# Attention scores in a graph kernel: eight multiply-and-sum instructions of 64 columns per step in place of one product over 512 columns and one sum

## The chip, the cores and the metric

The kernel runs on one core of one Trainium2 chip. The metric is the device time of the whole program in microseconds (us). The core has five engines that run side by side and meet only through semaphores: TensorE (PE in the profile), VectorE (DVE), ScalarE (ACT), GpSimd (POOL) and SyncE (SP). Each takes its instructions in the order in which they are written. In front of each engine stands a sequencer that reads the instructions, does register work and semaphore waits, and hands the rest on.

## The reference

The program is one graph-attention layer (with its own feed-forward part) and, behind it, a mixture of eight experts over the same 3,125 nodes of 256 features. The change touches the scores of the attention alone: for each of 53,125 edges and each of 4 heads, the product of a query row and a key row of 64 numbers each is summed.

```python
qi = q[dst]                                   # [53125, 4, 64]
kj = k[src]
vj = v[src]
alpha = jnp.sum(qi * kj, axis=-1) / jnp.sqrt(jnp.float32(D))      # D = 64
m = jax.ops.segment_max(alpha, dst, num_segments=n)
ex = jnp.exp(alpha - m[dst])
denom = jax.ops.segment_sum(ex, dst, num_segments=n)
a = ex / (denom[dst] + 1e-16)
out = jax.ops.segment_sum(a[..., None] * vj, dst, num_segments=n)
```

## The kernel before

There are four stages, one behind the other: `project` makes the rows of keys and values and sorts out which edges belong to which block of 128 nodes; `attend` runs over the edges; `mlp` and `experts` are dense layers, mostly products on TensorE. The change is in `attend`.

`attend` walks over 232 steps of 256 edges (`LT` = 2 tiles of 128 edges, one edge per partition). Eight steps (`CP`) make a chunk, four chunks (32 steps, `RING`) a round. The first round is written out, six rounds are a loop on each engine (`Fori(1, ROUNDS)`), and the last 8 steps and the tail of the pipeline are written out again. The work of one step, by engine:

- POOL fetches two tiles of key-and-value rows from HBM by index (`indirect_dma_start`, L665) into `ring`. It may run 8 steps ahead: it waits on `s_prod` for the step whose slot it refills. Once a chunk it also copies the indices (`idx`, L649) and the run starts (`stc`), after waits on `s_alpha` and `s_mp`.
- PE expands the queries of the block to one row per edge (six products into `psQ`, L735; four buffers, `NQ`, freed by `s_prod`), and 16 steps later sums the weighted values per node (`psA`, L758).
- DVE does the scores. L940 multiplies `psQ` (in PSUM) by the keys in `ring`, 128 partitions by 512 columns, into `prod`. L980 sums `prod` over runs of 64 columns into 8 numbers per partition: 2 tiles by 4 heads. Between the two stand other pieces of the step: parts of the running maximum over the previous chunk (`maximum`, parts 0, 1 and 2), the one-hot rows `oh` (L958), and the addition of `psA` to the result `acc` (L974, named `k_acc` in the trace). Once a chunk come the mask `ohT` (L827) and the rescaling of `acc` (L998).
- ACT takes the exponents and scales the values (eight instructions, L715).

At the start of every step DVE's sequencer loads the number of the block from memory into a register (`value_load`), which L974 of that step uses; the instructions behind it are handed on only after that. The order on each engine is written out by hand; nothing is scheduled by a planner. DVE writes a step in this order (parts left out):

```python
blk = nc.vector.value_load(brow[0:1, bass.ds(b, 1)], min_val=0, max_val=NB - 1)
...
dve.wait_ge(s_kv[jj], 16 * LT * (cc + 1))
dve.wait_ge(s_qe, step + 1)
...                          # product, L940
maximum(i, j, 0)
...                          # one-hot rows, L958
maximum(i, j, 1)
...                          # addition to acc, L974
maximum(i, j, 2)
...                          # sum, L980
```

In the first round DVE and ACT also split the projected queries into three parts (`remainder`, `lowest`, L833 and L837), one block per step.

Of the kernel before, what the change touches and what calls it, by code (L numbers as in the profile page):

```python
# [37 lines left out]
LT = 2  # L38
# [465 lines left out]
def attend(nc, ctx, io, keep):  # L504

    c = ExitStack()
    with c:
# [6 lines left out]
        def sem(name):  # L514
            return ctx.enter_context(nc.semaphore(name))
# [48 lines left out]
        s_oht, s_noh = sem("s_oht"), sem("s_noh")  # L564
        s_qe, s_prod, s_alpha = sem("s_qe"), sem("s_prod"), sem("s_alpha")
        s_mv, s_mp = sem("s_maxv"), sem("s_maxp")
# [70 lines left out]
        def _(pool):  # L637
            def at(i, j, fresh):
# [4 lines left out]
                if j % CP == 0:  # L643
                    if not (fresh and j < 2 * CP):
                        pool.wait_ge(s_alpha, CP * (cc - 1))
                        held(pool, s_turn[1])
                        pool.wait_ge(s_mp, NT * (cc - 2) + T_IN)
                        held(pool, s_turn[1])
# [169 lines left out]
        def _(dve):  # L818
# [28 lines left out]
            def maximum(i, j, part):  # L847
# [11 lines left out]
                if at == (0, 0):  # L859
                    dve.wait_ge(s_alpha, CP * m + CP)  # L860
                    nc.vector.tensor_tensor(alm[:, :, :], alpha[:, mpar, :, :],
                                            valN[:, bass.ds(W * m, W)].unsqueeze(1).broadcast_to([P, H, W]), ALU.add).then_inc(s_mv, 1)
# [64 lines left out]
            def at(i, j, fresh):  # L927
# [6 lines left out]
                if live(i, j, fresh):  # L934

                    dve.wait_ge(s_kv[jj], 16 * LT * (cc + 1))
                    dve.wait_ge(s_qe, step + 1)
                    if not (fresh and j < 2):
                        dve.wait_ge(s_alpha, step - 1)
                    nc.vector.tensor_tensor(prod[:, j % 2, :].rearrange("p (k d) -> p k d", k=LT),  # L940
                                            psQ[j % NQ][:, :].rearrange("p (k d) -> p k d", k=LT),
                                            ring[:, LT * jj:LT * jj + LT, q + 1, 0:HID], ALU.mult).then_inc(s_prod, 1)
                if now:
# [31 lines left out]
                if now:  # L975
                    maximum(i, j, 2)
                if live(i, j, fresh):

                    dve.wait_ge(s_prod, step + 1)
                    nc.vector.tensor_reduce(alpha[:, q % 2, :, LT * jj:LT * jj + LT].rearrange("p h w -> p w h"),  # L980
                                            prod[:, j % 2, :].rearrange("p (k h d) -> p k h d", k=LT, h=H), AX.X, ALU.add
                                            ).then_inc(s_alpha, 1)
                if fresh and QEARLY + j < NB:
# [831 lines left out]
```

## Time and profile before

| what | value |
|---|---|
| time, median of 3 runs | 1516.69 us (1516.41 to 1521.55) |
| profiled execution, its own time | 1517.29 us |
| its span, first to last instruction | 1515.5 us |
| DVE busy over the span | 1104.2 us (73%), 2825 instructions |
| PE busy | 1272.6 us (84%) |
| POOL busy | 848.6 us (56%) |
| ACT busy | 773.8 us (51%) |
| first L940 and last L980 | 110.9 us and 755.3 us |
| mean granted TensorE clock | 0.950 |

The shares are means over stages with different limits, so they say little about `attend`, which lies between some 110 and 780 us. What bounds it is read from the views of that stretch alone. A row of the timeline gives the start, the time from the start of the operation to its acknowledged end, and the instruction. On DVE one instruction often starts before the recorded end of the one before it, so the time that an instruction takes from the engine is the distance between two starts, and not its recorded length.

### The profile page before, as it was taken

The numbers are of one execution on the slowest core, as the hardware profiler recorded it, in microseconds if no ns is written. First come the engines' busy times: TensorE is split into PE (matmuls) and PEld (weight loads), VectorE is DVE, ScalarE is ACT, GpSimd is POOL, SyncE is SP. The second block draws the span as 40 slices with busy tenths as digits, with TensorE's granted clock in tenths as the row PEclk, the third lists the DMA queues.
The fourth block names the chain that finished last, engine by engine and source line by source line (L and its number), as shares of the span: only waits on it lengthen the run. The fifth ranks groups of instructions, "written<-read, shape, count | busy, mean of one in ns | idle before, by whom it ended". The sixth has DMA issues, their size and how long they took to land. (4 is left out here: it accounts for less than half of the span.)

```text
span 1515.5 us, 29900 instructions
## 1 busy us (share of the span) xinstructions
PE 1272.6 (84%) x7188; PEld 992.9 (66%) x7189; DVE 1104.2 (73%) x2825; ACT 773.8 (51%) x2480; POOL 848.6 (56%) x932
## 2 busy tenths in 40 slices
PE   5899777776767767777749999968899999999998
PEld 2434455454544545545537777757799999999998
DVE  4647999898988989988973555457956656566665
ACT  1155877786776767776732222213334435344443
POOL 2146777777777777777610111025656657566665
PEclk8999999899999999999988999968999999999999
DMA  5377777777777777777630111141110010100000
GB/s 182 117 220 221 223 215 204 214 221 217 205 216 206 209 217 216 212 210 214 172 108 22 53 52 52 33 136 42 60 36 19 1 52 0 35 17 0 18 2 16
DMA packets 83555, 184.24 MB, mean 122 GB/s; under 512 B 11611, under 2 KB 46262, under 8 KB 83454
## 3 DMA queue, kind: packets, MB, share of 16 engines
q0 software_dynamic: 37632, 124.28, 28.9%
q1 hardware_dynamic: 44438, 57.57, 11.5%
q10 hardware_dynamic: 1384, 1.32, 0.3%
q8 instruction: 31, 0.51, 0.1%
q14 instruction: 70, 0.57, 0.1%
HBM read 165.93 MB, written 17.18 MB: 121 GB/s over the span
## 5 line engine op out<-in xcount | busy, mean ns | idle before, releaser
L665 POOL DMA_INDIRECT ring<-kv_rows,idx x464 | 477.7, 1029 | 167.7 <-issue 127.7
L715 ACT ACTIVATE ring<-ring 128x64 f32<-128x64 f32 x1800 | 435.7, 335 | 0.9
L1533 ACT ACTIVATE hf<-psF,k_scT 128x320 f32<-128x320 f32 x320 | 197.8, 618 | 223.6 <-PE psF L1566 215.2
L735 PE MATMUL psQ<-k_q,ohT 128*128 x1392 | 210.3, 286 | 90.1 <-issue 89.9
L758 PE MATMUL psA<-ring,oh 128*128 128x260 f32 x928 | 255.3, 400 | 3.8 <-DVE k_acc L974 3.7
L735 PEld LDWEIGHTS psQ<-k_q,ohT 128*128 128x128 bf16 x1392 | 122.3, 99 | 148.5 <-issue 122.8
L1500 POOL TENSOR_TENSOR h2l<-hf,h2h 128x320 fp32r<-128x320 f32 x160 | 148.7, 944 | 115.2 <-DVE h2h L1709 115.2
L940 DVE TENSOR_TENSOR prod<-psQ,ring 128x512 f32<-128x512 f32 x232 | 158.6, 684 | 60.0 <-DMA ring<-kv_rows,idx 34.0
L758 PEld LDWEIGHTS psA<-ring,oh 128*128 128x128 f32 x928 | 166.5, 200 | 26.2 <-issue 4.2
L1500 POOL TENSOR_TENSOR h1l<-hf,h1h 128x320 fp32r<-128x320 f32 x160 | 148.3, 950 | 59.9 <-DVE h1h L1709 59.9
L980 DVE TENSOR_REDUCE alpha<-prod 128x8 f32<-128x512 f32 x232 | 155.8, 671 | 0.2
L1709 DVE CAST h2h<-hf 128x320 fp32r<-128x320 f32 x160 | 90.7, 583 | 62.7 <-ACT hf L1533 62.6
L1709 DVE CAST h1h<-hf 128x320 fp32r<-128x320 f32 x160 | 83.7, 529 | 56.3 <-ACT hf L1533 56.1
L1566 PE MATMUL psO<-wh,h2l 128*128 128x256 f32 x400 | 110.7, 297 | 9.2 <-DVE o L1698 8.4
L1698 DVE SCALAR_TENSOR_TENSOR o<-psO,wt,o 128x256 f32<-128x256 f32 x200 | 92.6, 479 | 33.4 <-PE psO L1566 32.1
L1566 PE MATMUL psO<-wl,h2h 128*128 128x256 f32 x400 | 107.3, 289 | 0.0
L1566 PE MATMUL psF<-xh,wl 128*128 128x320 f32 x320 | 100.9, 322 | 0.0
L1566 PE MATMUL psF<-xl,wh 128*128 128x320 f32 x320 | 99.7, 318 | 0.0
L1566 PE MATMUL psF<-h1h,wl 128*128 128x320 f32 x320 | 97.6, 313 | 0.0
L1566 PE MATMUL psF<-h1l,wh 128*128 128x320 f32 x320 | 96.3, 309 | 0.0
L974 DVE TENSOR_TENSOR k_acc<-k_acc,psA 128x260 f32 x232 | 93.7, 404 | 2.8 <-PE psA L758 1.0
L1130 POOL TENSOR_SCALAR ve<-mv 128x5 f32<-128x5 f32 x10 | 3.3, 329 | 164.7 <-DVE mv L1254 100.1
(234 smaller groups left out, 2332.4 us busy)
## 6 DMA issues: line engine op xcount, KB each, us to landing
ohT<-step_destinations SPq DMA_DIRECT2D x29, 512.0 KB, 4.3
ring<-kv_rows,idx POOLq DMA_INDIRECT x464, 3.8
kv_rows<-kvst SPq DMA_DIRECT2D x25, 260.0 KB, 2.1
we<-in_L_ffn_W SPq DMA_DIRECT2D x16, 256.0 KB, 3.0
residual<-qst SPq DMA_DIRECT2D x25, 128.0 KB, 3.6
resin<-residual SPq DMA_DIRECT2D x5, 640.0 KB, 6.6
after_graph_layer<-x SPq DMA_DIRECT2D x5, 640.0 KB, 5.7
xres<-after_graph_layer SPq DMA_DIRECT2D x5, 640.0 KB, 4.4
```

The costliest lines, as they stand in the source:

```text
L665: nc.gpsimd.indirect_dma_start(out=ring[:, LT * (j % CP) + k, j // CP:j // CP + 2, :].rearrange("p t e -> p (t e)"), out_offset=None, in_= ...
L715: last = nc.scalar.activation(row[:, 0:D], row[:, 0:D], ACT.Copy, scale=row[:, D:HW_])
L735: last = nc.tensor.matmul(psQ[j % NQ][:, k * HID:(k + 1) * HID], ohT[par][:, w * P:(w + 1) * P], q3[:, part, bass.ds(blk, 1), :].rearrange ...
L758: last = nc.tensor.matmul(psA[sj % NA][0:BP, 0:HALFW], oh[:, sj % NO, k, :], ring[:, LT * (sj % CP) + k, sj // CP, :], start=(k == 0), sto ...
L940: nc.vector.tensor_tensor(prod[:, j % 2, :].rearrange("p (k d) -> p k d", k=LT), psQ[j % NQ][:, :].rearrange("p (k d) -> p k d", k=LT), ri ...
L974: nc.vector.tensor_tensor(row, row, psA[sj % NA][0:BP, 0:HALFW], ALU.add).then_inc(s_acc, 1)
L980: nc.vector.tensor_reduce(alpha[:, q % 2, :, LT * jj:LT * jj + LT].rearrange("p h w -> p w h"), prod[:, j % 2, :].rearrange("p (k h d) -> ...
L1500: nc.gpsimd.tensor_tensor(low, hf[:, n, 0:b - a], high, ALU.subtract).then_inc(s_rl, 1)
L1533: nc.scalar.activation(hf[:, n, 0:b - a], psF[n][:, 0:b - a], ACT.Relu, bias=scT[:, 2 * layer - 1, col + m:col + m + 1], scale=scT[:, 2 * ...
L1566: mm = nc.tensor.matmul(out, ws(k)[iw], xs(k)[ix], start=(at == 0), stop=(at == len(n) - 1))
L1698: nc.vector.scalar_tensor_tensor(out=o[:, u, :], in0=ps, scalar=wt[:, u, e:e + 1], in1=o[:, u, :], op0=ALU.mult, op1=ALU.add).then_inc(s_c ...
L1709: nc.vector.tensor_copy(high, hf[:, n, 0:b - a]).then_inc(s_rh, 1)
```

## The change

The product and the sum become eight instructions, each of which multiplies 64 columns of `psQ` by 64 columns of `ring`, writes the products to `prod`, and writes their sum to one column of `alpha`. They stand together where the product stood. The semaphore `s_prod` is now signalled once, behind the last of the eight, and takes the place of `s_alpha` for those that waited for the sums.

```diff
@@ gpsimd @@
-                        pool.wait_ge(s_alpha, CP * (cc - 1))
+                        pool.wait_ge(s_prod, CP * (cc - 1))
@@ maximum, part 0 of a chunk's first step @@
-                    dve.wait_ge(s_alpha, CP * m + CP)
+                    dve.wait_ge(s_prod, CP * m + CP)
@@ vector, at(i, j, fresh) @@
                     dve.wait_ge(s_kv[jj], 16 * LT * (cc + 1))
                     dve.wait_ge(s_qe, step + 1)
-                    if not (fresh and j < 2):
-                        dve.wait_ge(s_alpha, step - 1)
-                    nc.vector.tensor_tensor(prod[:, j % 2, :].rearrange("p (k d) -> p k d", k=LT),
-                                            psQ[j % NQ][:, :].rearrange("p (k d) -> p k d", k=LT),
-                                            ring[:, LT * jj:LT * jj + LT, q + 1, 0:HID], ALU.mult).then_inc(s_prod, 1)
+                    for k in range(LT):
+                        for h in range(H):
+                            a = h * D
+                            last = nc.vector.tensor_tensor_reduce(
+                                out=prod[:, j % 2, k * HID + a:k * HID + a + D], in0=psQ[j % NQ][:, k * HID + a:k * HID + a + D],
+                                in1=ring[:, LT * jj + k, q + 1, a:a + D], scale=1.0, scalar=0.0, op0=ALU.mult, op1=ALU.add,
+                                accum_out=alpha[:, q % 2, h, LT * jj + k:LT * jj + k + 1])
+                    last.then_inc(s_prod, 1)
...
-                if live(i, j, fresh):
-
-                    dve.wait_ge(s_prod, step + 1)
-                    nc.vector.tensor_reduce(alpha[:, q % 2, :, LT * jj:LT * jj + LT].rearrange("p h w -> p w h"),
-                                            prod[:, j % 2, :].rearrange("p (k h d) -> p k h d", k=LT, h=H), AX.X, ALU.add
-                                            ).then_inc(s_alpha, 1)
```

In the built program each `tensor_tensor_reduce` is two DVE instructions: the one that multiplies and sums, and one that reads the sum out into a single column of `alpha`. The rows below are DVE's, from the second step of a chunk (j % 8 = 1) to the start of the third, in the kernel before. `ISA x2`, `REGISTER_ALU` and rows with a wait alone are the sequencer's; `TENSOR_LOAD k_brow` is the load of the block number.

```order
L958 ISA [waits s_agg]
L958 TENSOR_TENSOR oh<-k_iotaF,k_dstR 128x256
L974 ISA [waits s_rescaled,s_acc,s_agg]
L974 TENSOR_TENSOR k_acc<-k_acc,psA 128x260
L980 TENSOR_REDUCE alpha<-prod 128x2x4 [waits s_prod]
L933 ISA
L933 TENSOR_LOAD k_brow
L933 ISA x2
L937 REGISTER_ALU [waits s_kv2]
L940 TENSOR_TENSOR prod<-psQ,ring 128x512 [waits s_alpha,s_qe]
```

The same place in the changed kernel, where L961 and L977 are the former L958 and L974; the pair of rows of L941 stands eight times in a row.

```order
L961 ISA [waits s_agg]
L961 TENSOR_TENSOR oh<-k_iotaF,k_dstR 128x256
L977 ISA [waits s_rescaled,s_acc,s_agg]
L977 TENSOR_TENSOR k_acc<-k_acc,psA 128x260
L933 ISA
L933 TENSOR_LOAD k_brow
L933 ISA x2
L937 REGISTER_ALU [waits s_kv2]
L941 ISA prod,alpha<-psQ,ring 128x64 [waits s_qe]
L941 ISA alpha 128x1
```

The sum of 512 columns no longer stands between the addition to `acc` and the load of the block number; 16 instructions stand behind the load where one stood. On POOL nothing moves, and only the semaphore's name changes, as in this piece of the difference at the start of a chunk in the loop (the copy of the indices and the wait ahead of it):

```order
 L665 DMA ring<-kv_rows,idx 128x520
 L645 REGISTER_ALU
-L647 ISA [waits s_alpha]
+L647 ISA [waits s_prod]
 L649 ISA [waits s_maxp]
 L649 COPY idx<-k_srcI 128x16
```

The waits of PE and POOL on `s_prod` for a free buffer stay where they were; the signal itself now comes behind the last sum.

## Rows read from the trace of the kernel before

**Rows 1.** The page, costliest groups: the product and the sum.

```profile
L940 DVE TENSOR_TENSOR prod<-psQ,ring 128x512 f32<-128x512 f32 x232 | 158.6, 684 | 60.0 <-DMA ring<-kv_rows,idx 34.0 <-issue 20.7 <-DVE alpha L980 2.2
L980 DVE TENSOR_REDUCE alpha<-prod 128x8 f32<-128x512 f32 x232 | 155.8, 671 | 0.2
```

**Rows 2.** Busy time by window: four rounds of the loop, second and sum.

```profile
core 0: us, PE busy (x) PEld busy (x) DVE busy (x) ACT busy (x) POOL busy (x), PEclk, DMA share, GB/s
375.75:466.26 90.51, 65.28 (x372) 44.26 (x372) 79.02 (x217) 64.67 (x268) 67.94 (x72) 0.96 0.74 212
sum 360.14, PE 267.06 PEld 180.27 DVE 316.49 ACT 258.70 POOL 269.69; mean PE 66.77 PEld 45.07 DVE 79.12 ACT 64.68 POOL 67.42
```

**Rows 3.** DVE's waits, 120 to 780 us: total, times, longest.

```profile
DVE prod L940 <- DMA ring<-kv_rows,idx: 34.0, 36, 2.8
DVE prod L940 <- issue: 20.7, 10, 4.1
DVE qst L833 <- ACT k_q L683: 5.5, 6, 1.4
DVE prod L940 <- DVE alpha L980: 2.2, 6, 0.5
```

**Rows 4.** DVE's timeline around 412 us: start, length, line, instruction.

```profile
411.56 0.67 DVE L980 TENSOR_REDUCE alpha<-prod 128x8 f32<-128x512 f32 x1
412.16 0.67 DVE L940 TENSOR_TENSOR prod<-psQ,ring 128x512 f32<-128x512 f32 x1
412.75 0.20 DVE L919 TENSOR_TENSOR dif<-alm,psM 128x64 f32<-128x64 f32 x1
412.88 0.41 DVE L958 TENSOR_TENSOR oh<-k_iotaF,k_dstR 128x256 f32<-128x256 f32 x1
...
419.23 0.69 DVE L940 TENSOR_TENSOR prod<-psQ,ring 128x512 f32<-128x512 f32 x1 [2.05 <-DMA ring<-kv_rows,idx]
```

**Rows 5.** POOL's timeline: first gathers of two chunks in a row.

```profile
413.50 1.30 POOL L665 DMA_INDIRECT ring<-kv_rows,idx  x1 [1.04 <-DVE prod L940]
415.10 0.95 POOL L665 DMA_INDIRECT ring<-kv_rows,idx  x1 [0.30 <-issue]
416.36 0.94 POOL L665 DMA_INDIRECT ring<-kv_rows,idx  x1 [0.30 <-issue]
...
436.22 1.30 POOL L665 DMA_INDIRECT ring<-kv_rows,idx  x1 [1.04 <-DVE prod L940]
```

**Rows 6.** DVE's timeline, short instructions in a row.

```profile
410.25 0.27 DVE L909 TENSOR_SCALAR oh<-k_iotaF,k_dstR 1x128 f32<-1x128 f32 x1
410.45 0.14 DVE L912 COPY bin_<-psR 64x1 f32<-64x1 f32 x1
410.52 0.40 DVE L958 TENSOR_TENSOR oh<-k_iotaF,k_dstR 128x256 f32<-128x256 f32 x1
```

**Rows 7.** DVE's timeline, four and five short instructions merged.

```profile
22.84 0.36 DVE L354 BATCH_NORM_AGGREGATE mv<-st 128x2 f32<-128x6 f32 x4
...
788.29 0.66 DVE L1254 BATCH_NORM_AGGREGATE mv<-st 128x2 f32<-128x6 f32 x5 [0.15 <-DVE st L1249]
```

**Rows 8.** DVE's timeline, a sum directly behind its product.

```profile
119.54 0.68 DVE L940 TENSOR_TENSOR prod<-psQ,ring 128x512 f32<-128x512 f32 x1
120.25 0.69 DVE L980 TENSOR_REDUCE alpha<-prod 128x8 f32<-128x512 f32 x1
```

**Rows 9.** DVE's timeline, instructions around loads of the block number.

```profile
408.84 0.67 DVE L980 TENSOR_REDUCE alpha<-prod 128x8 f32<-128x512 f32 x1
409.50 0.69 DVE L940 TENSOR_TENSOR prod<-psQ,ring 128x512 f32<-128x512 f32 x1
...
421.24 0.42 DVE L998 TENSOR_TENSOR k_acc<-k_acc,fac 128x260 f32 x1
421.78 0.69 DVE L940 TENSOR_TENSOR prod<-psQ,ring 128x512 f32<-128x512 f32 x1
```

**Rows 10.** DVE's timeline, the first product of a round.

```profile
466.26 0.69 DVE L940 TENSOR_TENSOR prod<-psQ,ring 128x512 f32<-128x512 f32 x1 [3.67 <-issue]
```

More of the change, by code:

```diff
@@ L564, in attend @@
         s_oht, s_noh = sem("s_oht"), sem("s_noh")
-        s_qe, s_prod, s_alpha = sem("s_qe"), sem("s_prod"), sem("s_alpha")
+        s_qe, s_prod = sem("s_qe"), sem("s_prod")
         s_mv, s_mp = sem("s_maxv"), sem("s_maxp")
```

## The prediction

> **What bounds the kernel now.** The change lives in `attend`, so I read the group table first, to see how often its two instructions run: 232 products of 684 ns and 232 sums of 671 ns [rows 1]. Next I took the busy time of four rounds of the loop, to see which engine is fullest there. A round lasts 360.14 / 4 = 90.0 us. DVE is busy for 79.1 us of it, POOL for 67.4, PE for 66.8 and ACT for 64.7 [rows 2]. DVE is therefore the fullest by busy time, with 10.9 us of idle time a round. DVE's waits say what that idle time is: in `attend` 34.0 us for the gathered rows to arrive and 20.7 us of "issue", in which nothing in the profile is waited for [rows 3]. The issue time sits mostly at the loop's back edge, with 3.67 us ahead of a round's first product [rows 10]; there are five such places, of 3.6 to 4.1 us.
>
> The wait for rows has a second engine behind it. POOL starts a gather every 1.26 us, since 0.30 us of issue lies ahead of each, and 22.72 us lie between the first gathers of two chunks [rows 5]. Sixteen gathers at 1.26 are 20.2 us, and the copies and the wait at the head of a chunk are the rest. DVE needs 79.1 / 4 = 19.8 us for a chunk, and it catches up with POOL about once a chunk, as in the 2.05 us ahead of the product at 419.23 [rows 4]. So two engines set the pace nearly together: DVE with its instructions and its back edge, 79.1 + 4 = 83 us a round, and the gathers with some 88 us. Whatever DVE gains is lost to the gathers, and what it loses is free only for the first 5 us a round or so. That matters more here than the shares of the whole span.
>
> **What is removed.** The price of an instruction in a full queue is the distance between starts. The sum at 411.56 is followed by the product at 412.16, and that by the next instruction at 412.75 [rows 4]. That is 0.60 and 0.59 us, so a step gives back 1.20 us. The wait for `s_alpha` ahead of the product and that for `s_prod` ahead of the sum go too. In a steady step both had long been met, so I cost them at nothing.
>
> **What is added.** Sixteen instructions a step: eight of 64 columns that read PSUM and SBUF, and eight that write one column. The trace has neither kind under its own name. For the first the nearest row is `dif`, 64 columns from PSUM and SBUF, with 412.88 - 412.75 = 0.13 us between starts [rows 4]. A 128-column instruction takes 0.20 and a one-column copy from PSUM takes 0.07 [rows 6], whose middle is 0.135. For the second the nearest row is that one-column copy, at 0.07. A pair then costs 0.205 us and eight pairs 1.64 us. This is the lower bound: it supposes that the readout starts without waiting for the end of the sum, and that the sequencer keeps up.
>
> Whether it keeps up is the first open cost. Four tiny instructions behind long ones took 0.36 us together, so (0.36 - 0.15) / 3 = 0.07 each, but five that came behind an idle moment took 0.66, so (0.66 - 0.15) / 4 = 0.127 each [rows 7]. I read the first as instructions that stood ready and the second as the pace at which they can be handed on. Sixteen in a row are more than were ever seen to stand ready, and at 0.127 they take 2.03 us. A block thus costs 1.64 to 2.03 us. I take the middle, 1.82, since the long instructions ahead of the block let the sequencer run ahead for its first part only. Against the 1.20 removed that is +0.62 us a step.
>
> **The Trainium skill on the same price.** The row says 0.13 us for 64 columns out of PSUM [rows 4]. The Trainium skill, page "VectorE: DVE Perf Modes", section on the TRN2 errata, charges 120 cycles plus one per column for a PSUM source and 58 plus one for an SBUF source, at 0.96 GHz. By an estimate from that page a pair is 0.192 + 0.061 = 0.253 us, eight are 2.03 us, and with the rest of my sum unchanged the program would take 1686 us. The row disagrees with the PSUM figure (0.13 against 0.19), and I go by the row.
>
> **What is moved.** The sum of `prod` stood between the addition to `acc` and the load of the block number, and its 0.60 us hid that load. Even that was barely enough: at 408.84, behind very short instructions, the next product came 0.66 us later and not 0.60. Behind the rescaling at 421.24, with a load of its own just before it, it came 0.54 us later [rows 9], where instructions of that width otherwise follow each other at 0.34. So a load that has only an addition of 260 columns over it can show through by up to 0.20 us. In the new order that addition always stands there, but no load directly ahead of it; so 0 to 0.20, and I take 0.08 us a step. Together the step grows by 0.62 + 0.08 = 0.70 us on DVE, which is 232 x 0.70 = 162 us.
>
> The signal `s_prod` comes 1.2 us later within the step. PE has four `psQ` buffers and POOL eight steps of `ring`, so both keep at least three steps of cover, some 8 us. I cost it at nothing; without that cover it would be up to 1.2 us a step. ACT's and PE's 65 to 67 us a round leave them far from binding.
>
> **What is absorbed.** With DVE slower than the gathers, its waits for them vanish: 34.0 us, with 2.2 that are put down to the sum of the step before. In the first round DVE also waits 5.5 us behind ACT's splitting of the queries, and that covers the longer block there [rows 3]. That makes 41.7 us. The 20.7 us of issue stay. The code of a round grows by 14 instructions a step, and if fetching at the five back edges doubled with it, that would be 18 us more [rows 10]. I leave this out of the sum and in the range.
>
> **Sum.** On the profiled execution's own time: 1517.3 + 162 - 41.7 = 1638 us. The runs' median lies 0.6 below that execution, so I say 1637. By rounds: 79.1 + 32 x 0.70 + 4.1 = 105.6 us against 90.0, over 7.25 rounds 113 us, which agrees.
>
> **The rivals.**
>
> *The readout waits for the end of its sum.* A sum waited for by semaphore started 0.71 us behind the start of a product that lasted 0.68, that is 0.03 behind its end [rows 8]. If the engine holds the readout back in the same way, a pair is 0.20 (the recorded length of 64 columns) + 0.03 + 0.07 = 0.30 us, and eight are 2.40. The step grows by 1.28 us, so 297 - 42 = +255, about 1772 us. For it speaks that the readout needs the last column's sum. Against it speaks that the overlap of 0.07 to 0.08 us between neighbours looks like the acknowledgement of the write, which the readout does not need. The Trainium skill, page "VectorE: DVE Perf Modes", section on two Vector instructions with no wait between them, counts an instruction that writes out its accumulator as two and holds one back only when start quadrants differ. All operands here start at partition 0, so by that rule nothing is held; no run so far shows it.
>
> *Everything one after the other.* If the next sum also waits for the readout's recorded end, the pair is 0.23 + 0.14 + 0.03 = 0.40 us, eight are 3.2, the step grows by 2.08 us, and the time is 1517 + 483 - 42 = 1958 us.
>
> *Not slower: the gathers hide it.* The block may grow by 41.7 / 232 = 0.18 us a step before the time moves, since DVE then only fills its waits for POOL. That needs a pair of no more than (1.20 + 0.18) / 8 = 0.17 us with the load hidden. A 64-column instruction of 0.135 leaves 0.04 for the readout, below the 0.07 of the shortest instruction in the trace. If the readout cost nothing at all, DVE would gain 0.12 us a step and the gathers would keep it: the time would stay within a few us of 1517.
>
> **How the numbers follow.** Pairs of 0.205 to about 0.26 us with my other terms: 0.58. The readout waits: 0.24. Everything in turn: 0.12. Hidden by the gathers: 0.05, of which 0.01 falls to a gain. The last 0.01 is for costs outside these. The likeliest case spans 1517 + 232 x 0.44 - 42 = 1577 (lower bound, load hidden) to 1517 + 232 x (0.83 + 0.20) - 42 = 1714, and with the back edges 1732. The range runs from 1565 to 1785 so as to take in the waiting readout; outside lie the fully serial case and the hidden one. Faster, the same and slower, at a bound of 0.5%, are 0.01, 0.04 and 0.95; 0.5% is about what a measurement of this kernel can tell.
>
> **What would show it.** In the new profile the 232 rows each of L940 and L980 are replaced by 1856 pairs. I expect starts of pairs 0.20 to 0.25 us apart, blocks of about 1.8 us, a round of about 106 us, DVE busy for nearly all of it, no waits for gathered rows, and POOL waiting on `s_prod` in every step. Ahead of each block I expect a short issue gap of about 0.1 us. The prediction is wrong if pairs lie 0.3 us apart or more, if the gap ahead of each block is several tenths, or if the back edges have grown.

## The result and the profile after

The changed kernel takes 1565.03 us (median of 4 runs, 1564.44 to 1571.32) against 1516.55 us (1516.06 to 1521.55) of the kernel before: a ratio of 1.0332, 95% interval 1.0305 to 1.036. It is slower by 48 us, where 120 were forecast. The profiled span is 1563.8 us. The granted clock is 0.963 and was 0.950, so the clock is no cause. A ratio is always against the kernel before of the same series of measurements, since that kernel took 1513 to 1519 us in some series, called quiet below, and 1621 to 1636 us in others, called busy, for a reason that isn't known and that is not the chip, as some expectations guess (chips 8 and 11 each gave both).

The page of the changed kernel, costliest groups (columns as in [rows 1]), has the 1856 pairs in place of the product and the sum:

```profile
L941 DVE CUSTOM_DVE_ANT_0 prod<-psQ,ring 128x64 f32<-128x64 f32 x1856 | 289.2, 220 | 91.3 <-issue 82.3
L941 DVE DVE_READ_ACCUMULATOR2_ANT alpha<- 128x1 f32 x1856 | 153.2, 83 | 1.0 <-issue 0.2
```

By these sums the pairs cost 442 us where product and sum cost 314. That reading is wrong, since the recorded ends overlap. The timeline of the changed kernel around 430 us gives the distances between starts:

```profile
428.71 0.39 DVE L977 TENSOR_TENSOR k_acc<-k_acc,psA 128x260 f32 x1
429.03 0.20 DVE L879 COPY inh<-carry 1x64 f32<-1x64 f32 x1
429.69 0.22 DVE L941 CUSTOM_DVE_ANT_0 prod<-psQ,ring 128x64 f32<-128x64 f32 x1 [0.47 <-issue]
429.84 0.08 DVE L941 DVE_READ_ACCUMULATOR2_ANT alpha<- 128x1 f32 x1
429.84 0.22 DVE L941 CUSTOM_DVE_ANT_0 prod<-psQ,ring 128x64 f32<-128x64 f32 x1
429.98 0.08 DVE L941 DVE_READ_ACCUMULATOR2_ANT alpha<- 128x1 f32 x1
...
430.85 0.08 DVE L941 DVE_READ_ACCUMULATOR2_ANT alpha<- 128x1 f32 x1
430.85 0.14 DVE L882 COPY cin<-psR 64x1 f32<-64x1 f32 x1
430.92 0.41 DVE L961 TENSOR_TENSOR oh<-k_iotaF,k_dstR 128x256 f32<-128x256 f32 x1
...
431.64 0.39 DVE L977 TENSOR_TENSOR k_acc<-k_acc,psA 128x260 f32 x1
431.96 0.41 DVE L889 TENSOR_TENSOR_SCAN B<-nrow,F 64x128 f32<-64x128 f32 x1
432.62 0.23 DVE L941 CUSTOM_DVE_ANT_0 prod<-psQ,ring 128x64 f32<-128x64 f32 x1 [0.25 <-issue]
...
434.90 0.14 DVE L904 TENSOR_TENSOR fd<-tails,back 1x4 f32<-1x4 f32 x1
435.57 0.22 DVE L941 CUSTOM_DVE_ANT_0 prod<-psQ,ring 128x64 f32<-128x64 f32 x1 [0.53 <-issue]
```

Two things are to be seen. First, a readout starts at the very moment at which the next sum starts (429.84 twice), and takes nothing from it. A pair is 0.145 us and the block of eight goes from 429.69 to 430.85, 1.16 us, which is also the median of all blocks. The 1.20 us that were removed paid for it. Second, ahead of each block there is a stop with nothing waited for. From the small copy `inh` to the block it is 0.66 us, where such a copy is followed at 0.10 in places without a load. It is 0.66 behind `B` (0.33 without a load) and 0.67 behind `fd` (0.08). Between these instructions and the block stand the load of the block number with its range check, and semaphore waits, to none of which the view puts these stops down.

The trace also has the sequencer's own rows (DVEq), with the shortest, the median and the longest in ns. These are the ones of the load in the changed kernel, 120 to 830 us:

```profile
L933 DVEq FUSED_REGOPS  x394: 53/190/190, 159.9 to 829.9; - x197
L933 DVEq TENSOR_LOAD <-k_brow x232: 297/307/329, 159.6 to 829.5; - x116
L933 DVEq SEQ_ASSERT  x231: 23/23/23, 160.2 to 829.1; - x116
```

The load itself is 0.31 us, and behind it stand 0.19 and 0.02 us of range check (the rows of 53 ns stand ahead of it). By the starts of these rows, the block starts 0.76 to 0.84 us behind the start of the load at each of the eight steps of a chunk (medians by step), whatever instruction stands last. The load itself starts between 0.32 us before and 0.11 us after that last instruction. In the kernel before it starts 0.14 to 0.76 us before the sum at the seven steps where the sum stands last, and the sum's 0.60 us then run over the rest of it.

The waits of DVE in the changed kernel, 120 to 830 us, have it in one line, against 10 times and 20.7 us in [rows 3]:

```profile
DVE prod L941 <- issue: 82.3, 169, 5.0
DVE k_acc L995 <- DVE k_acc L977: 11.5, 28, 0.6
```

The second line is the rescaling: it has a load of its own, which the sum covered before and which now stands directly behind the addition. No line for gathered rows is left; 34.0 us stood there before. The busy time by window, four rounds of the loop in the changed kernel, second and sum as in [rows 2]:

```profile
397.53:496.13 98.60, 64.79 (x372) 43.55 (x372) 80.58 (x665) 64.78 (x268) 66.31 (x72) 0.98 0.68 195
sum 392.59, PE 260.79 PEld 174.72 DVE 323.18 ACT 259.15 POOL 264.22; mean PE 65.20 PEld 43.68 DVE 80.79 ACT 64.79 POOL 66.06
```

A round takes 392.59 / 4 = 98.15 us and took 90.04: 8.1 us more. I split both rounds by distances between starts on DVE. The instructions themselves come to some 77.3 us and were 78.4. Stops for the load, with those inside the blocks, are some 16.5 us and were 1.4. Waits for gathered rows are 0 and were 6.1. The back edge is 4.5 and was 3.9 (4.57, 4.48, 4.96, 4.63 and 3.70 us at the five places). That gives -1.1 + 15.1 - 6.1 + 0.6 = 8.5, near the 8.1 measured. The loss is one item, and part of it was absorbed.

### The profile page after: what moved, and what is told of

The parts are those of the page before. It is cut to its first block and busy times, and to the rows that moved or that the text cites. A ratio compares the mean times of both kernels' runs of the same rounds, so it can differ in the third digit from the quotient of the medians.

```text
span 1563.8 us, 32956 instructions
## 1 busy us (share of the span) xinstructions
PE 1261.1 (81%) x7188; PEld 982.9 (63%) x7189; DVE 1110.3 (71%) x6073; ACT 775.1 (50%) x2480; POOL 835.9 (53%) x932
## 5 line engine op out<-in xcount | busy, mean ns | idle before, releaser
L665 POOL DMA_INDIRECT ring<-kv_rows,idx x464 | 464.9, 1002 | 198.1 <-issue 127.1
L941 DVE CUSTOM_DVE_ANT_0 prod<-psQ,ring 128x64 f32<-128x64 f32 x1856 | 289.2, 220 | 91.3 <-issue 82.3
L735 PE MATMUL psQ<-k_q,ohT 128*128 x1392 | 205.1, 281 | 113.7 <-issue 96.3
L758 PE MATMUL psA<-ring,oh 128*128 128x260 f32 x928 | 249.3, 393 | 3.3 <-DVE k_acc L977 3.0
L758 PEld LDWEIGHTS psA<-ring,oh 128*128 128x128 f32 x928 | 161.8, 195 | 28.4 <-issue 6.5
L941 DVE DVE_READ_ACCUMULATOR2_ANT alpha<- 128x1 f32 x1856 | 153.2, 83 | 1.0 <-issue 0.2
L961 DVE TENSOR_TENSOR oh<-k_iotaF,k_dstR 128x256 f32<-128x256 f32 x232 | 95.4, 411 | 0.0
L977 DVE TENSOR_TENSOR k_acc<-k_acc,psA 128x260 f32 x232 | 93.4, 403 | 2.0 <-PE psA L758 1.0
```

Of the source, the lines that this page charges most:

```text
L665: nc.gpsimd.indirect_dma_start(out=ring[:, LT * (j % CP) + k, j // CP:j // CP + 2, :].rearrange("p t e -> p (t e)"), out_offset=None, in_= ...
L735: last = nc.tensor.matmul(psQ[j % NQ][:, k * HID:(k + 1) * HID], ohT[par][:, w * P:(w + 1) * P], q3[:, part, bass.ds(blk, 1), :].rearrange ...
L758: last = nc.tensor.matmul(psA[sj % NA][0:BP, 0:HALFW], oh[:, sj % NO, k, :], ring[:, LT * (sj % CP) + k, sj // CP, :], start=(k == 0), sto ...
L941: last = nc.vector.tensor_tensor_reduce(out=prod[:, j % 2, k * HID + a:k * HID + a + D], in0=psQ[j % NQ][:, k * HID + a:k * HID + a + D], ...
L961: nc.vector.tensor_tensor(oh[:, sj % NO, :, :], iotaF[:, 0:BP].unsqueeze(1).broadcast_to([P, LT, BP]), dstR[:, bass.ds(LT * bo, LT)].unsqu ...
L977: nc.vector.tensor_tensor(row, row, psA[sj % NA][0:BP, 0:HALFW], ALU.add).then_inc(s_acc, 1)
```

## The experiments

The theory to test (cover theory): DVE's sequencer starts the load only when it has handed on the instruction ahead. It comes there hardly ahead of the engine, so nothing long is queued by then. The 0.60 us of the removed sum used to hide the load. The rival: 14 more instructions a step cost time in themselves, in issue or in fetching.

### The order alone

The kernel before, with the sum of step j-1 directly behind the product of step j. No instruction is added, but the load now stands behind the same small instructions as in the changed kernel.

```diff
@@ vector, behind the product @@
+                if not (fresh and j == 0) and (live(i, j, fresh) or (isinstance(i, int) and RING * i + j == STEPS)):
+                    jb = (j - 1) % RING
+                    qb, jjb = jb // CP, jb % CP
+                    dve.wait_ge(s_prod, step)
+                    nc.vector.tensor_reduce(alpha[:, qb % 2, :, LT * jjb:LT * jjb + LT].rearrange("p h w -> p w h"),
+                                            prod[:, jb % 2, :].rearrange("p (k h d) -> p k h d", k=LT, h=H), AX.X, ALU.add
+                                            ).then_inc(s_alpha, 1)
@@ vector, end of the step @@
-                if live(i, j, fresh):
-
-                    dve.wait_ge(s_prod, step + 1)
-                    nc.vector.tensor_reduce(alpha[:, q % 2, :, LT * jj:LT * jj + LT].rearrange("p h w -> p w h"),
-                                            prod[:, j % 2, :].rearrange("p (k h d) -> p k h d", k=LT, h=H), AX.X, ALU.add
-                                            ).then_inc(s_alpha, 1)
```

> The kernel before, with the sum over the product of step j-1 placed directly behind the product of step j; nothing is left out, and the same instructions run. The addition to acc now stands directly ahead of the load of the block number, as in the changed kernel. Cover theory: the changed kernel is slow because the 0.60 us sum no longer hides the load, so this one should show the same gap of some 0.3 us ahead of each product (0.67 us from the start of the addition to the start of the product) and take 1550 to 1565 us. Sequencer theory: the changed kernel is slow because DVE's sequencer has 14 more instructions to hand on in each step and never gets ahead; here it has no more than before, runs ahead during product and sum, and the time stays at 1517 to 1525 us.

> The kernel before with the sum of step j-1 directly behind the product of step j, again, since its first run met the slower chip; nothing is left out. There its trace already had 0.69 us from the start of the last short instruction to the product, where 0.08 to 0.33 would be the distance without a load. Summed over a round that is some 11 us of idle time, of which the gathers' slack takes 6. Cover theory: on a chip that runs the kernel before in 1517 us this takes 1545 to 1560 us, a ratio of 1.02 to 1.03, with no change in any instruction. If the number of instructions is what counts, the ratio is below 1.005.

> The kernel before with the sum of step j-1 moved directly behind the product of step j, so that what stands ahead of the load of the block number in the next step is the same short instruction as in the changed kernel, while the scores are still one product and one sum: no instruction is added. Alone in its call. If the loss of the changed kernel is the uncovered load of the block number (cover theory), this kernel loses most of it too: distances of 0.65 to 0.7 us from the last short instruction to the product, 9 to 13 us more a round less what the gathered rows gave (6 a round), 1545 to 1565 us, ratio 1.02 to 1.03. If the loss comes from the number of instructions (14 more a step), it stays within 0.5% of the kernel before: 1512 to 1525 us.

The first two were in busy series: 1627.66 against 1623.08 us, ratio 1.0019 (0.9993 to 1.0045), and 1624.37 against 1621.24, ratio 1.001 (0.9983 to 1.0037). The stops were there (0.69 to 0.70 us behind `inh` and `fd`), the total didn't show them. The third was in a quiet one: **1560.22 against 1518.33 us, ratio 1.0269 (1.0213 to 1.0324)**. The timeline of that run, around 409 us:

```profile
409.68 0.21 DVE L902 TENSOR_TENSOR iv<-back,k_nxt 1x64 f32<-1x64 f32 x1
409.82 0.14 DVE L904 TENSOR_TENSOR fd<-tails,back 1x4 f32<-1x4 f32 x1
410.52 0.69 DVE L940 TENSOR_TENSOR prod<-psQ,ring 128x512 f32<-128x512 f32 x1 [0.56 <-issue]
411.12 0.68 DVE L947 TENSOR_REDUCE alpha<-prod 128x8 f32<-128x512 f32 x1
```

It stops 0.70 us behind `fd` like the changed kernel, with the old instructions. So the order alone costs 42 us, where the change costs 48. The two are not made of quite the same pieces. Here the load is still covered at two of eight steps: it starts 1.04 and 1.12 us ahead of the addition that stands last, against 0.17 and 0.24 in the changed kernel, which loses some 0.5 us a chunk more by it. In return this order has a wait that the changed kernel has not: once a chunk `alm` waits for the sum directly ahead of it and starts 0.82 us behind it, where other instructions start 0.59 behind, which is some 7 us of the 42. The waits of that run, 120 to 830 us:

```profile
DVE prod L940 <- issue: 76.4, 143, 3.8
```

### Fewer loads

The changed kernel and the kernel before, each with the block number loaded once a chunk. Seven of eight steps then add to a block that isn't chosen by their own number: that choice is left out.

```diff
+            kept = []
...
-                    blk = nc.vector.value_load(brow[0:1, bass.ds(b, 1)], min_val=0, max_val=NB - 1)
+                    if jj == 0 or (fresh and j == ADD_LAG) or not kept:
+                        kept[:] = [nc.vector.value_load(brow[0:1, bass.ds(b, 1)], min_val=0, max_val=NB - 1)]
+                    blk = kept[0]
```

> The changed kernel with the block number for the addition loaded once in eight steps instead of in each; the seven steps behind it add to the block of the first, so the choice of the block is left out for them. Both theories: with seven of eight loads gone the gap ahead of the block goes, the issue idle falls from 82 to some 30 us, and the gathers set the pace: 1505 to 1520 us. If the load is not the cost and the sixteen instructions are slow to fetch or to hand on by themselves, the time stays above 1545 us.

> The changed kernel with one load of the block number a chunk, again on what I hope is the chip of the first measurement; the choice of the block is left out for seven steps of eight. Cover theory: all but one in eight of the stops go, some 14 of 15 us a round, the gathers set the pace, and the time is 1500 to 1520 us (ratio 0.99 to 1.00). If the instructions themselves are supplied too slowly, gaps appear inside the blocks and the ratio stays at 1.02 or more.

> The changed kernel with one load of the block number a chunk instead of one a step, again; the choice of the block is left out for seven steps of eight. Where instructions are supplied fast enough: no gap ahead of the blocks, ratio to the kernel before 0.99 to 1.005. Where they are not: the gaps move into the blocks and the ratio stays near that of the changed kernel. If the load is not the cost, the ratio equals that of the changed kernel on either chip.

> The kernel before with one load of the block number a chunk for its addition, instead of one a step; the choice of the block is left out for seven steps of eight. In the kernel before the load is hidden behind the sum of 0.60 us, so the time stays within 1% of the kernel before, whose pace the gathers set. If loads cost there too, it gains more than 1%.

> The changed kernel with one load of the block number a chunk, run alone this time, since the kernel before took 1517 us where one kernel was sent alone and 1620 to 1636 us in all runs of several together. The choice of the block is left out for seven steps of eight. If the stops for the load are the whole loss: 1500 to 1520 us, a ratio of 0.99 to 1.00. If the loss is in the supply of the instructions: gaps inside the blocks, a ratio of 1.02 or more.

The quiet series decides for the result: **1506.11 against 1517.54 us, ratio 0.9933 (0.9907 to 0.9958)**. With seven of eight of these loads gone the changed kernel takes 0.7% less than the kernel before, a small difference but clear of its interval. The distances to the block fall to 0.10 behind `inh`, 0.08 behind `fd` and 0.33 behind `B`, and the gathered rows are waited for again. DVE's waits, 120 to 830 us:

```profile
DVE prod L945 <- issue: 28.4, 6, 6.0
DVE prod L945 <- DMA ring<-kv_rows,idx: 15.5, 12, 3.1
```

In busy series it is otherwise. There this kernel took 1689.06 against 1623.08 us (1.039), 1687.22 against 1621.24 (1.0412) and 1706.92 against 1636.07 (1.0432, 1.0399 to 1.0464), though its stops ahead of the blocks are gone. The kernel before with one load a chunk took 1639.67 against 1636.07 (1.0005, 0.9977 to 1.0032). So in busy series taking the loads away gives nothing that can be seen, and the kernel with the pairs stays 4% behind.

> The changed kernel itself, beside the next two on the same chip, since the first four experiments met a chip on which the kernel before took 1623 us instead of 1517. If the loss is a fixed amount of work on DVE, the ratio to the kernel before is 1.03 on any chip. If it is a matter of how fast instructions are supplied, the ratio on the slower chip is larger, 1.04 to 1.08, with issue idle inside the blocks.

The changed kernel, run unchanged in that same series, took 1702.18 against 1636.07 us, 1.0393 (1.0357 to 1.0429). DVE's waits of that run, 120 to 830 us, name a place that the quiet run hardly has, a stop between sum and readout (alpha, 0.2 us in all in the page above):

```profile
DVE prod L941 <- issue: 99.2, 181, 4.4
DVE alpha L941 <- issue: 30.9, 47, 1.2
```

This looks like the rival theory, that the instructions come too slowly, but the runs don't show it. The same pairs at the end of the step cost only 1.4 to 1.7% in busy series, and with twice the pairs the stops between sum and readout were fewer (25.4 us in 52 places against 37.4 in 56, over the whole of `attend`; both edits follow). What costs the 4% in busy series is open.

### The block at the end of the step

The eight pairs stand where the sum stood, so that they should cover the load of the next step.

> The changed kernel, with the block of eight pairs moved from the head of the step to its end, where the sum stood; nothing is left out. Cover theory: the block of 1.16 us now stands between the addition and the load of the block number and hides the load, so the issue idle falls to some 25 us and the time to 1510 to 1525 us. Sequencer theory: the order does not matter, since the sequencer works through the 16 short instructions about as slowly as the engine does and arrives at the load with nothing queued; the time stays at 1555 to 1575 us and the gap only moves to the instruction behind the load.

> The changed kernel with the block at the end of the step, again. With the range check kept, the sequencer stops behind the block, whose last instructions take 0.07 us each, so only what stands ready covers the stop. From the trace of the version without the check (96.0 us a round against 98.2 of the changed kernel) I expect 1550 to 1565 us, a ratio of 1.02 to 1.03. If a block of 1.16 us covered the stop as the sum of 0.60 did, it would be 1510 to 1520 us.

> The changed kernel with both remedies: the block of pairs at the end of the step, where the sum stood, and the block number of the addition loaded without its range check, so that nothing stops for it before the addition; nothing is left out. If stopping for the load is what the change costs, this one loses it all: on the chip of the first measurement 1500 to 1520 us, where the gathers set the pace, and on the slower chip a ratio of 1.00 to 1.01 against 1.039 of the changed kernel. If the number of instructions is the cost, the ratio stays at 1.03 or above.

Both runs with the range check were in busy series: 1647.91 against 1623.08 us, 1.014 (1.0095 to 1.0185), and 1648.91 against 1621.24, 1.0168 (1.0132 to 1.0203). That is some 2.4% less than the changed kernel of such a series. The third also leaves the range check away (the load without `min_val` and `max_val`) and was in a quiet series: 1549.97 against 1517.52 us, 1.0209 (1.0182 to 1.0237). I had expected more of it. Its timeline around 433 us shows where the stops went:

```profile
433.36 0.15 DVE L829 TENSOR_SCALAR noh<-ohT 128x1 f32<-128x1 bf16 x1
433.88 0.42 DVE L965 TENSOR_TENSOR k_acc<-k_acc,psA 128x260 f32 x1 [0.37 <-issue]
```

Without bounds at the load, the check is made where the number is used: the sequencer's rows of up to 0.19 and of 0.02 us now belong to the line of the addition, which followed `noh` at 0.19 us and now follows at 0.52. The experiment had moved a stop, not removed it.

> The changed kernel with the block number of the addition loaded in every step but without its range check, so that the first instruction that needs the loaded number is the addition itself and not the check directly behind the load; nothing of the computation is left out. If the load only costs because the sequencer stops for its answer, the gap ahead of the block shrinks from 0.3 us to 0.1 or less and the time falls to 1505 to 1530 us. If the load itself holds the sequencer, or if the number of instructions is what counts, the time falls by less than 20 us, to 1545 or more. A stop that moves to the addresses of the addition would show as idle time ahead of the addition.

> The changed kernel with the load of the block number in its own place, only without the two range checks on the number. Alone in its call, for the share of the checks in the 48 us. Earlier it ran among others, where its distances from the last short instruction to the pairs were 0.36 us against 0.66 us with checks. By that, 0.3 us a step or up to 9 us a round comes back at the steps where nothing else waits: 1525 to 1550 us, ratio 1.005 to 1.02. If the place alone makes the cost, it stays at 1555 to 1570 us.

The same edit in the changed order was measured twice, both times in busy series: 1684.16 against 1623.08 us, 1.0339 (1.0287 to 1.0391), and 1693.27 against 1634.12, 1.0366 (1.0316 to 1.0416). Its distances from `inh`, `B` and `fd` to the block are 0.36 to 0.37 us where they were 0.66, and from the start of the load to the block it is 0.48 where it was 0.77. So some 0.3 us of the stop is the check. What is left of it is 0.26 behind `inh` (0.36 less the 0.10 without a load), 0.30 behind `fd` and 0.04 behind `B`. Here too the check came back ahead of the addition, which follows `noh` at 0.52 us. The total of this version in a quiet series wasn't measured.

### Twice the pairs

Every pair is issued twice; the first eight write to buffers that nobody reads (`pr` and `al` take the places of `prod` and `alpha`).

```diff
-                    for k in range(LT):
+                    for pr, al, k in [(prod2, alpha2, k) for k in range(LT)] + [(prod, alpha, k) for k in range(LT)]:
...
```

> The changed kernel with every pair issued twice, the first eight into buffers that nobody reads; nothing is left out. It prices eight pairs in a queue that is already running. At 0.145 us a pair, as in the trace of the changed kernel, a step grows by 1.16 us and the program by 232 x 1.16 = 269 us, a ratio near 1.21. If the sequencer falls behind in a long run of short instructions, as the prediction had it, a pair costs 0.20 to 0.25 and the ratio is 1.28 to 1.34.

It took 1870.99 us against 1636.07 in a busy series, 1.1428 (1.1375 to 1.1481). I had expected a ratio near 1.21. The block of sixteen takes 2.37 us in the median, 0.148 a pair. The sequencer therefore keeps up with at least 32 instructions in a row at 0.074 us each. That settles the price of the pair. The total is 169 us above the changed kernel of the same series and not 232 x 1.2 = 278; some of the block presumably lay beside other stops of that series, which no run separates.

### How a load is hidden

Three more versions are complete and without the range check at load or use. First, seven loads in a row behind the first block of a chunk, kept in registers (`number`, a load without its check, is shown with the next version).

```diff
...
+                if jj == 0 and not fresh:
+                    for t in range(1, CP):
+                        if live(i, j + t, fresh, ADD_LAG):
+                            kept[j + t] = number(step + t - ADD_LAG)
```

> The changed kernel, complete, but the block numbers of a chunk's next seven steps are loaded one behind the other right behind the chunk's first block of pairs and kept in seven registers, without range checks; the rescale takes its number from there too where it lies in them. The question is whether seven loads in a row cost seven stops or one. If each waits for the one before (0.35 us or more each), a chunk loses 2.5 us in one place, 10 us a round, and the kernel stays near 1545 to 1560 us, ratio 1.02 or more. If they overlap, a chunk loses some 0.5 to 0.8 us in one place, and the kernel comes to what the version with one load a chunk took plus a few us: 1503 to 1518 us, ratio 0.992 to 1.0.

It took 1552.53 against 1515.26 us, 1.0255 (1.0238 to 1.0273). The timeline at such a place:

```profile
340.98 0.09 DVE L947 DVE_READ_ACCUMULATOR2_ANT alpha<- 128x1 f32 x1
344.13 0.23 DVE L861 TENSOR_TENSOR alm<-alpha,k_valN 128x64 f32<-128x64 f32 x1 [3.06 <-issue]
```

Seven loads stop DVE for 3.06 us, or 0.44 each. They don't overlap: the sequencer's rows show each at 0.30 to 0.34 us, and none starts before the one ahead has ended.

Then one load a step, for the next step, directly behind this step's block. The rescaling takes the number that is already there.

```diff
+            def number(b):
+                return nc.s_assert_within(nc.vector.value_load(brow[0:1, bass.ds(b, 1)]), 0, NB - 1,
+                                          skip_runtime_bounds_check_because="the plan holds block numbers below NB")
...
-                    blk = nc.vector.value_load(brow[0:1, bass.ds(b, 1)], min_val=0, max_val=NB - 1)
+                    blk = kept.pop(j) if j in kept else number(b)
...
                     last.then_inc(s_prod, 1)
+                    if j + 1 < RING and live(i, j + 1, fresh, ADD_LAG):
+                        kept[j + 1] = number(step + 1 - ADD_LAG)
...
-                    blk = nc.vector.value_load(brow[0:1, bass.ds(br, 1)], min_val=0, max_val=NB - 1)
+                    blk = kept[j + 1] if j + 1 in kept else number(br)
```

> The changed kernel, complete, but the block number of the next step is loaded right behind this step's block of pairs and kept in a register, without range checks, and the rescale uses the number that is already there. One load a step as before the edit, only in another place. If a load stops VectorE wherever the work queued ahead of it is short (cover theory: the block of pairs is issued at nearly the engine's pace, so little is queued), the stop moves behind the block at 0.3 to 0.4 us: 1530 to 1550 us, ratio 1.01 to 1.02. If only the short instruction ahead and the check made it dear, it is hidden: below 1517 us.

It took **1497.18 against 1513.09 us, 0.9896 (0.9842 to 0.995)**, less than I had expected and less than both kernels, 1% below the kernel before. Its timeline, around 405 us:

```profile
405.05 0.07 DVE L947 DVE_READ_ACCUMULATOR2_ANT alpha<- 128x1 f32 x1
405.29 0.21 DVE L893 COPY heads<-psR 1x64 f32<-1x64 f32 x1 [0.17 <-issue]
405.45 0.43 DVE L969 TENSOR_TENSOR oh<-k_iotaF,k_dstR 128x256 f32<-128x256 f32 x1
...
406.46 0.14 DVE L904 TENSOR_TENSOR fd<-tails,back 1x4 f32<-1x4 f32 x1
406.53 0.20 DVE L947 CUSTOM_DVE_ANT_0 prod<-psQ,ring 128x64 f32<-128x64 f32 x1
```

The block follows `fd` at 0.07 us. Behind the block the load shows as 0.17 us here. In the median over the loop it shows as nothing at two of the eight steps and as 0.08 to 0.30 us at the other six, 4.4 us a round in all, where the uncovered loads cost some 16.5. The sequencer is ahead of the engine by part of the block when it comes to the load, which is enough for most of the cover and not for all. The waits and the windows of four rounds (sum) of this kernel:

```profile
DVE prod L947 <- issue: 18.8, 5, 4.1
...
sum 350.73, PE 259.23 PEld 175.52 DVE 318.41 ACT 259.13 POOL 260.91; mean PE 64.81 PEld 43.88 DVE 79.60 ACT 64.78 POOL 65.23
```

Ahead of the blocks only the five back edges are left of the issue time, and a round is 350.73 / 4 = 87.7 us. DVE waits for gathered rows only 2.6 us in all, so DVE sets this pace and not the gathers.

Last, the same load in the kernel before, behind its product.

> The kernel before, complete, with the same load of the block number one step ahead, without range checks, here right behind the product (0.60 us on VectorE). It says whose gain the version with the pairs and the load ahead has. Before has its load behind the sum, where it costs 0.60 us from the sum to the next product in 0.60 us of sum, nothing; behind the product of 0.60 us it should be covered as well (0.35 to 0.4 us without a check). So the cover theory expects no more than 0.5% from the kernel before, 1510 to 1520 us. If range checks or the placing help any kernel by themselves, this one gains the same 1% as the pairs with the load ahead did: 1495 to 1503 us.

It took 1515.97 against 1517.11 us, 0.9992 (0.9969 to 1.0016): no change. Its waits for gathered rows are 49.8 us, against 34.0:

```profile
DVE prod L946 <- DMA ring<-kv_rows,idx: 49.8, 35, 3.2
DVE prod L946 <- issue: 6.9, 2, 3.5
```

Most of that growth is a matter of names: three back edges of 2.9 to 3.2 us are put down to the rows here and stood under "issue" before. Without them the waits for rows are 40.5 us, 6.5 more. DVE gained about as much: the product follows the rescaling at 0.34 us in place of 0.54, once a chunk, some 6 us in all. So what DVE gained there, it waited for POOL. The 1% of the version above comes with the pairs, given that their load is hidden. Why that version isn't held back by the gathers in the same way is open in part. Its chunks of gathers start 22.1 us apart in the median, against 22.7 in the kernel before, and the difference lies at the head of a chunk: the last gather ahead of it takes 0.95 us in the median and took 1.52, and the first behind it 0.97 and 1.30. No run says why.

## Why the prediction was right and wrong

**The direction, and what bounds.** DVE and the gathers set the pace nearly together, and the change put DVE behind: right. The waits for rows vanished as forecast, 34.0 and 2.2 us [rows 3].

**What is removed.** 1.20 us a step: right, by the same way of reading starts.

**Sixteen instructions a step: this step failed.** I took 1.82 us for the block, 1.64 to 2.03. It measured 1.16, so the term is -0.04 us a step in place of +0.62. Even my lower bound charged each readout 0.07 us of its own, as if it were a one-column copy [rows 6]. The readout starts with the next sum and costs nothing. The upper bound came from the pace of five instructions behind an idle moment [rows 7] and took it for a steady pace; thirty-two in a row went at 0.074. The estimate from the Trainium skill, page "VectorE: DVE Perf Modes", section on the TRN2 errata, 0.253 us a pair, is further off still. The row of 64 columns alone, 0.13 [rows 4], was the pair's price within 0.015.

**What is moved: right mechanism, wrong size.** I saw that the sum covered the load and that the bound was 0.20 us a step, and took 0.08. The runs give some (16.5 - 1.4) / 32 = 0.47 a step. That also is a step that failed, and the trace has the sign of being wrong that the prediction had named, a gap of several tenths ahead of each block. I read the bound from the two places in [rows 9] where 0.60 us of sum, or an addition, still lay over the load. I said that in the new order the addition always stands there. It doesn't: in three of eight steps a piece of the maximum (`inh`, `B`, `fd`) stands last. Such a piece, or `iv` ahead of `fd`, waits for a result of the instruction ahead of the addition, which holds the sequencer back, and the load starts only 0.1 us ahead of the piece. I had looked at the order at one of the steps without such a piece. There the forecast failed too: from an addition that stands last to the block it is 0.67 us in the median, where 0.33 is usual. The cause is the same by the sequencer's rows, since the block starts 0.76 to 0.84 us behind the start of the load there as well. Why the sequencer isn't further ahead at those steps no run separates.

**Absorbed, back edges.** Of the 41.7 us, the 36.2 at the product went. The 5.5 behind ACT's splitting of the queries did not: that wait is 7.1 us in the same stretch. The back edges grew by 0.6 us and not by 3.7.

**The sum.** I charged the load to all 232 steps, but the first 17 blocks have none ahead of them. With the measured terms it is 215 x 0.47 - 232 x 0.04 = 92, less 36.2, some +56 us; the result was +48, and the rest is not accounted for. The two errors, 0.66 us a step too much for the block and 0.39 too little for the load, partly cancelled. So the forecast of 1637 missed by 72 us and not by more, and it is luck that the result still lies at the edge of the range.

**The rivals.** The readout that waits and the serial chain are refuted by the two rows at 429.84. The rival with gathers hiding it had the right price, a readout for nothing, and failed by the load, which it took as hidden. Once the load is covered the runs come close to it: 1506 us with one load a chunk, 1497 with the load a step ahead. It forecast that the gathers would keep the gain, but 1% remained.

A figure that I hadn't weighed: the Trainium skill, page "DMA: Bandwidth & Descriptors", section "Latency and other measured facts", gives a `tensor_load` a floor of about 600 ns. The load with its check shows 0.66 us from a small copy that takes 0.10, which is near that. Without the check the same distance is 0.36, seven in a row were 0.44 each, and the sequencer's row of the load is 0.31, so as a floor for the load alone it doesn't hold here. Looking for it would have shown that the load term could not be 0.08 wherever the cover is gone.

## What to carry to other kernels

A register load on an engine's own sequencer is paid for by work already queued behind it on the engine. Before moving or shortening an instruction, list which loads it covers, at every step of the pattern and not at one; ahead of an instruction that waits for a fresh result the sequencer has stood still, so such an instruction gives little cover. Where a change takes that cover away, load one step ahead, behind a run of instructions that wait for nothing, and look where the range check goes.

Price a fused instruction by distances between starts. The group table said 442 us against 314 here where the cost was equal.

Compare only with a kernel before of the same series: in busy ones the same edits ranked otherwise (order alone 1.00 in place of 1.03, fewer loads 1.04 in place of 0.99). Whether the best version also loses there wasn't tried.

## What the hardware did that I had not expected

The readout of the accumulator has a row of 83 ns and takes no time of the engine: it starts with the next sum (429.84 twice). A load of one number into a register holds DVE's sequencer for 0.31 us, and a range check on it adds 0.3 us to the way to the next instruction. In a place without cover the two together stop the engine for 0.56 us behind a small copy (0.66 less 0.10), and the load alone for 0.26. Loads in a row aren't overlapped (3.06 us for seven). A check left away at the load comes back where the number is used (0.52 us from `noh` to the addition in place of 0.19), unless it is left away at both. In busy series the kernel with the pairs lost 4%, with stops in the middle of the blocks, and why is open.
